# Graph network layers: rows shared by neighbouring rounds of scatters are given over from two chunks instead of one

## The chip, the cores and the metric

The kernel runs on one core of a Trainium2 chip. The metric is the time of one execution on the device in microseconds (us); lower is better. Engines are named as in the profile: PE (TensorE), DVE (VectorE), ACT (ScalarE), POOL (GpSimd), SP (SyncE). All but DVE and PE also issue transfers here.

## The reference, cut to what matters

There are 50000 nodes and 25000 edges, each with 128 features in fp32. Two graph layers run one after the other, each with a residual:

```python
edge_index = stack([src, dst])              # dst is sorted, src is random
h = relu(layernorm(x))
x = x + SAGE(h)                             # mean of h[src] over edges with the same dst, @ W_l.T, + h @ W_r.T
h = relu(layernorm(x))
agg = segment_sum(edge_attr_128, src, 50000)
h = concat([h, agg], axis=1)
h = bn(silu(h @ W1 + b1)); h = bn(silu(h @ W2 + b2))
x = x + (h @ W3 + b3)
```

`bn` takes its mean and variance over all nodes. Of this the change touches the segment sum of the second layer alone: rows of `edge_attr` are multiplied by the lower half of W1 and added at row `src[e]` of a table in DRAM, `acc2`.

## The kernel before, in words

**Tiling.** Nodes and edges go in 49 rounds, 0 to 48: 512 edges and 1024 nodes in each, the last with a shorter tail. A round is written (i, par) with r = 2i + par. Its 512 edges are four chunks, c0 to c3 here, of 128 rows. The phases are A (first layer), B (second layer's sums, and its first product), C (adds `acc2`, silu, statistics), F and G.

**Scatters of B.** `scatter_b(k)` (L837) issues four indirect DMAs on the POOL queue (L848). Each adds 128 rows of 128 floats to `acc2` at the rows in `target_b`. An add is a read and a write of DRAM, so two scatters that hold the same row must not be in flight together. Inside a round this can't be: equal rows are summed beforehand into one of them, and the others are sent to rows past the table (`count`, `mark`, `aim`: more than one match moves the target to a dump row). Between rounds it is kept in order by waits: c0 of a round waits until c0, c1 and c2 of the round before have landed (`s_sc2`, 48), and c1 waits until its c3 has landed (`s_end2`, 16). c0 needn't wait for that c3: a row that c3 shares with c0 of the next round is given over to it. `compare_carry` (L1170) finds such rows (`carried`, L1177) and moves their old target to the dump row; in `edge_product` (L1434) PE adds c3 of the round before, through `carried`, to c0 of the new round (L1440).

**One round of B on each engine.** POOL: the four scatters. DVE, `body_b` (L1279) for round r: eight adds x1 = acc1 times 1/degree + y (L1291), eight `bn_stats` (L1296), `bn_aggr` (L1302), then for round r + 2 `match` (four `scalar_tensor_tensor` of 128, 256, 384 and 512 columns, L1153) and the carry, then the targets of round r + 1 (`aim`, L1143), then the scales of round r (L1194, L1195). ACT, `body_b` (L999): normalise r (eight, L904), copy z of r - 1 (L992), copy the sums of r + 2 (L919), relu of r (L912), the root of r + 1 (L897), copy the product of r + 2 (`copy_v`, L925) into one of four buffers. PE, `round_b` (L1481): sums of r + 2 (L1430), transposes of r (L1422), `edge_product` of r + 2 (L1438, L1440), product of r (L1495).

**SP's queue of B**, `step_b` (L600) for round r, in this order: wait until c3 of r has landed (L603); load acc1 (L506) for round r + 2, and from round 32 on its y too (the stretch from there on is called spilled: y of the rounds before is still on the chip, and the results z of later rounds go out to DRAM from ACT's queue, L997); wait for DVE's adds of r; store x1 of r (L514); load the names and the edge rows for r + 4 (L585, L588).

Of the kernel before, what the change touches and what calls it, by code (L numbers as in the profile page):

```python
# [7 lines left out]
P = 128  # L8
ROWS = 4
# [5 lines left out]
def this(sem, par, i, inc=1):  # L15

    return sem[par], (i + 1) * inc


def two_ago(sem, par, i, inc=1):  # L20

    return sem[par], i * inc


def four_ago(sem, par, i, inc=1):

    return sem[par], (i - 1) * inc


def last(sem, par, i, inc=1):  # L30

    return sem[1 - par], (i + par) * inc


def gnn_layers(nc, x, src, dst, edge_attr, WlT, WrT, W1, b1, g1, be1, W2, b2, g2, be2, W3, b3, out):
# [90 lines left out]
    with ctx:  # L126
        def sb(name, shape, dt=fp32):
            return ctx.enter_context(nc.sbuf_tensor(name, shape, dt))
# [4 lines left out]
        def pair(name):  # L133
            return [sem(f"{name}_{k}") for k in range(2)]
# [27 lines left out]
        def part(shape, dt=fp32):  # L162
# [8 lines left out]
            if dt is not fp32:  # L171
# [29 lines left out]
        sumT = part([P, ROWS, P])  # L201
        irow = part([P, 2, ROWS, P])
        iota_c = part([P, COLS // 2]).bitcast(fp16)
        carried = [iota_c[:, :].bitcast(fp32)[:, 0:P], tabs[:, 2 * GROUP:2 * GROUP + P]]
        cols = part([P, 2, 4, ROWS])
        count = sb("count", [P, 2, ROWS])
        more = sb("more", [P, 2])
        alone = sb("alone", [P, 2])
        shift = sb("shift", [P, 2, ROWS])

        st6 = part([P, 2, 12, 6])
# [6 lines left out]
        hot_dve = [spare[:, 2 * ACT_H * P:(ROWS + ACT_H) * P].rearrange("p (j c) -> p j c", j=ROWS - ACT_H),  # L218
                   w2s[:, :].bitcast(fp16).rearrange("p (j c) -> p j c", j=ROWS - ACT_H)]
        bst = sb("bst", [P, 2 * (RF + 1), 6])  # L220
        zeros = bst[:, :, :].rearrange("p a s -> p (a s)")[:, 0:ZCOLS]
        row_stage = hT[:, 1, :, :].rearrange("p c d -> p (c d)")[:, 0:4 * P].rearrange("p (k c) -> p k c", k=4)
        bn = sb("bn", [P, 2, 8])
# [26 lines left out]
        def phase(tag, names):  # L250

            return {k: pair(f"{tag}_{k}") for k in names.split()}
# [5 lines left out]
        s_pre = pair("pre_rows_loaded")  # L258
        B = phase("b", common.replace(" stored", "") + " rows_loaded y_loaded a_loaded z_copied z_stored")
        x1_stored = [sem(f"b_x1_stored_{k}") for k in range(RING)]  # L260
        C = phase("c", "transposed added silu stats stored")
        F = phase("f", "product silu stats stored")
        G = phase("g", "scaled product done stored early_stored")

        acc2_loaded = [pair(f"acc2_loaded_{k}") for k in range(2)]
        x1_loaded = [pair(f"x1_loaded_{k}") for k in range(2)]
# [1 line left out]
        late_loaded = [sem(f"late_loaded_{r}") for r in range(2 * KEPT_LATER, RF + 1)]  # L268
        s_sc1 = pair("acc1_scattered")
        s_sc2 = pair("acc2_scattered")  # L270
        s_end2 = pair("acc2_last_chunk_scattered")
        s_set = sem("eps_then_zeros_then_names_set")
        s_fetched = sem("z_fetched")
# [149 lines left out]
        def x1_place(i, par):  # L423

            if type(i) is int and not 2 <= i < IT - 1:
                return (xin if i in (0, IT - 1) else res)[:, par, :, :]
            return kept(i - 2, par)
# [66 lines left out]
        def _(sp):  # L494
# [125 lines left out]
            sweep(sp, step_b, (KEPT,), wide=True, margin=2)  # L620


            sp.wait_ge(*this(s_sc2, 0, IT, 48))
            sp.wait_ge(*this(s_sc2, 1, IT - 1, 48))
            sp.wait_ge(*this(s_end2, 0, IT, 16))
            sp.wait_ge(*this(s_end2, 1, IT - 1, 16))
            for k in range(RING):
# [120 lines left out]

            def store_out(i, par, tail=False, early=False):
                sp.wait_ge(*this(G["done"], par, i))  # L750
                store_nodes(x1_place(i, par), out_v, 2 * i + par, tail, G["early_stored" if early else "stored"][par])

            def step_g(i, half, odd, par, early=False):

# [8 lines left out]
            doubled(sp, lambda *step: step_g(*step, early=True), 3, EARLY_G)  # L763
            doubled(sp, step_g, EARLY_G, EARLY_G + 4)
            for par in range(2):
                sp.wait_ge(G["early_stored"][par], 16 * EARLY_G)
            for i, par, tail in late_rounds():
                load_late(zy_dram, KEPT_LATER, i, par, tail, kept(i - KEPT_LATER, par))
            doubled(sp, step_g, EARLY_G + 4, KEPT_LATER)
# [13 lines left out]
        def _(pool):  # L783
# [53 lines left out]
            def scatter_b(k):  # L837

                i, par = k // 2, k % 2
                pool.wait_ge(*this(B["v_copied"], par, i))  # L840
                pool.wait_ge(*this(B["targets"], par, i))

                if k:
                    pool.wait_ge(*last(s_sc2, par, i, 48))
                for j in range(ROWS):
                    if k and j == 1:
                        pool.wait_ge(*last(s_end2, par, i, 16))
                    pool.indirect_dma_start(  # L848
                        acc2, bass.IndirectOffsetOnAxis(ap=target_b[:, k, j:j + 1], axis=0),
                        vrow_b[k % RING][:, j, :], None, compute_op=ALU.add)\  # L850
                        .then_inc((s_end2 if j == ROWS - 1 else s_sc2)[par], 16)

            def fetched_a(k):

# [25 lines left out]
        def _(act):  # L880
# [53 lines left out]
            def copy_v_b(i, par, tail, slot):  # L934
                if type(i) is int and i == 0:
                    act.wait_ge(*this(s_sc1, 1 - par, IT - 1 + par, 64))
                elif type(i) is int and i == 1:
                    act.wait_ge(*this(s_sc1, 0, IT, 64))
                else:
                    act.wait_ge(*four_ago(s_sc2, par, i, 48))  # L940
                    act.wait_ge(*four_ago(s_end2, par, i, 16))
                copy_v(B, vrow_b[slot], i, par, tail)

# [131 lines left out]
        def _(dve):  # L1075
# [59 lines left out]
            def link_(ins):  # L1135
                signal(ins)
                settle()
# [32 lines left out]
            def compare_carry(i, par, tail):  # L1170

                p = edge_parts(tail)
                before = 1 - par
                match(B, i, par, tail)
                if not (type(i) is int and i == 0):
                    dve.wait_ge(*two_ago(B["v_ready"], par, i))
                link_(nc.vector.scalar_tensor_tensor(  # L1177
                    carried[par][:, 0:p], irow[:, par, 0, 0:p], cols[:, before, 0, ROWS - 1:ROWS],
                    alone[:, before:before + 1].broadcast_to([P, p]), ALU.is_equal, ALU.mult,
                    accum_out=more[:, par:par + 1]))  # L1180
                nc.vector.tensor_scalar(alone[0:p, par:par + 1], count[0:p, par, ROWS - 1:ROWS], 1.5, None, ALU.is_lt)
                link_(nc.vector.scalar_tensor_tensor(
                    count[:, before, ROWS - 1:ROWS], more[:, par:par + 1], 2.0, count[:, before, ROWS - 1:ROWS],
                    ALU.mult, ALU.add))
                link_(mark(before, False))
                dve.sem_inc(B["compared"][par], 1)
# [79 lines left out]
            dve.wait_ge(*this(A["summed"], 1, IT - 1))  # L1266
            for par in range(2):
                link_(nc.vector.tensor_copy(cols[:, par, 0:2, :], src_tab[:, par, :, :]))
                if par:
                    compare_carry(0, par, False)  # L1270
                else:
                    link_(match(B, 0, par, False))
                    link_(nc.vector.tensor_scalar(alone[:, par:par + 1], count[:, par, ROWS - 1:ROWS], 1.5, None,
                                                  ALU.is_lt))
                    dve.sem_inc(B["compared"][par], 1)
            aim(B, 0, 0, False)
            done[0] += chain["n"]
            add_a(IT, 0, True, 2, 0)
            def body_b(before, now, after, ahead):  # L1279
                i, par, tail, spill, slot = now  # L1280
                r = 2 * i + par
# [117 lines left out]
        def _(pe):  # L1399
# [34 lines left out]
            def edge_product(w, par, tail, carry=None):  # L1434
                p = edge_parts(tail)
                for j in range(ROWS):
                    given = carry is not None and j == 0
                    ins = nc.tensor.matmul(psV[0:p, j, :], sumT[:, j, 0:p], w[:, :], start=True, stop=not given)  # L1438
                    if given:
                        ins = nc.tensor.matmul(psV[0:p, j, :], carried[par][:, 0:p], carry[:, ROWS - 1, :],  # L1440
                                               start=False, stop=True)
                return ins

            def round_a(i, par, tail):
# [30 lines left out]
            def multiply_edges_b(i, par, tail, _, slot):  # L1475
                pe.wait_ge(*this(B["sum_copied"], par, i))
                pe.wait_ge(*last(B["v_copied"], par, i))
                first = type(i) is int and i == 0 and par == 0
                edge_product(w1b, par, tail, None if first else vrow_b[(slot - 1) % RING]).then_inc(B["v_ready"][par], 1)

            def round_b(before, now, after, ahead):  # L1481
# [100 lines left out]
```

## Time and profile before

| | |
|---|---|
| median of 3 runs | 1505.77 us (1505.55 to 1508.4) |
| the profiled execution's own time | 1503.21 us |
| its span in the trace | 1501.3 us |
| mean granted TensorE clock | 0.918 |
| busy: PE, DVE, ACT, POOL | 68%, 73%, 57%, 55% of the span |

Busy shares are means over phases with different limits, so the phase that the change touches has to be read by itself. In the trace B's scatters run from 650.9 to 1132.2 us. The profiled execution is 2.56 us below the median. A landing time is counted from the start of the instruction that issues the transfer.

### The profile page before, as it was taken

The numbers are of one execution on the slowest core, as the hardware profiler recorded it, in microseconds if no ns is written. First come the engines' busy times: TensorE is split into PE (matmuls) and PEld (weight loads), VectorE is DVE, ScalarE is ACT, GpSimd is POOL, SyncE is SP. The second block draws the span as 40 slices with busy tenths as digits, with TensorE's granted clock in tenths as the row PEclk, the third lists the DMA queues.
The fourth block names the chain that finished last, engine by engine and source line by source line (L and its number), as shares of the span: only waits on it lengthen the run. The fifth ranks groups of instructions, "written<-read, shape, count | busy, mean of one in ns | idle before, by whom it ended". The sixth has DMA issues, their size and how long they took to land.

```text
span 1501.3 us, 22959 instructions
## 1 busy us (share of the span) xinstructions
PE 1021.5 (68%) x5247; PEld 726.3 (48%) x5247; DVE 1099.7 (73%) x4644; ACT 862.9 (57%) x1686; POOL 828.5 (55%) x601
## 2 busy tenths in 40 slices
PE   0237767677666667658777777776657877997866
PEld 0125555555544455435444444444435765446755
DVE  1438888888867766669788878776764877778978
ACT  0226777777755555537666666656564545665533
POOL 6778887888888888766666667655551000000000
PEclk9959999999999988969999999889997998999989
DMA  9988898877766666677777777899987996207999
GB/s 277 386 275 220 204 228 211 187 166 169 170 146 142 135 144 143 140 159 199 196 195 197 193 195 198 234 264 273 268 247 250 348 333 234 97 28 260 407 403 373
DMA packets 225365, 333.72 MB, mean 222 GB/s; under 512 B 35778, under 2 KB 87242, under 8 KB 225300
## 3 DMA queue, kind: packets, MB, share of 16 engines
q1 hardware_dynamic: 157516, 285.22, 56.1%
q0 software_dynamic: 62720, 38.57, 20.4%
q10 hardware_dynamic: 5064, 9.29, 1.7%
q14 instruction: 52, 0.43, 0.1%
q8 instruction: 13, 0.21, 0.1%
HBM read 179.20 MB, written 153.80 MB: 222 GB/s over the span
## 4 chain that ended last, share of the span: by engine, by line
POOL 41%; DMA 26%; issue 16%; PE 10%; DVE 5%; SPq 1%; ACT 1%; POOLq 0%; DVEq 0%; ACTq 0%
POOL acc L833 20%; POOL acc L848 11%; DMA acc<-zT,target_b 8%; DMA acc<-tabs,target_b 8%; POOL xin L811 7%; PE ps L1538 6%; POOL zT L819 4%; DMA zT<-x_dram 3%; DMA xin<-acc 2%; PE ps L1548 1%; DMA acc<-zT,tabs 1%; DVE zT L1383 1%; DVE zT L1387 1%; PE ps L1514 1%; PE ps L1517 1%
## 5 line engine op out<-in xcount | busy, mean ns | idle before, releaser
L1430 PE MATMUL ps<-zT 128*128 128x512 f32 (+5 forms) x784 | 278.0, 505 | 196.4 <-ACT zT L951 135.4
L833 POOL DMA_INDIRECT acc<-zT,tabs x196 | 314.8, 1606 | 71.5 <-issue 64.6
L1430 PEld LDWEIGHTS ps<-zT 128*128 128x128 f32 (+1 forms) x784 | 162.6, 217 | 338.8 <-issue 208.8
L848 POOL DMA_INDIRECT acc<-zT,target_b x100 | 161.0, 1610 | 87.1 <-DMA acc<-zT,target_b 32.5
L1153 DVE SCALAR_TENSOR_TENSOR zT<-zT 128x128 f32<-128x128 f32 (+3 forms) x392 | 192.9, 548 | 12.7 <-DMA zT<-row_dram 6.4
L1221 DVE BATCH_NORM_STATS2 zT<-zT 128x6 f32<-128x128 f32 (+1 forms) x384 | 78.9, 278 | 165.3 <-DMA zT<-in_x_dram 165.3
L848 POOL DMA_INDIRECT acc<-tabs,target_b x96 | 153.7, 1601 | 81.4 <-issue 32.0
L811 POOL DMA_INDIRECT xin<-in_x_dram,tabs x140 | 141.9, 1014 | 47.3 <-issue 42.4
L1422 PE MATMUL ps<-ident,zT 128*128 128x128 f32 (+1 forms) x784 | 111.5, 288 | 65.4 <-ACT zT L904 65.4
L1422 PEld LDWEIGHTS ps<-ident,zT 128*128 128x128 f32 (+1 forms) x784 | 92.2, 149 | 78.4 <-ACT zT L904 75.7
L1548 PE MATMUL ps<-w,hT 128*128 128x128 f32 (+1 forms) x784 | 101.5, 285 | 38.2 <-DVE zT L1387 28.7
L1328 DVE BATCH_NORM_STATS2 bst<-zT (+1 forms) x168 | 107.5, 682 | 23.7 <-ACT zT L1048 23.7
L1461 PE MATMUL ps<-wr,hT 128*128 128x128 f32 (+1 forms) x784 | 102.4, 287 | 32.3 <-DVE zT L1212 32.0
L1461 PEld LDWEIGHTS ps<-wr,hT 128*128 128x128 f32 (+1 forms) x784 | 98.6, 201 | 40.0 <-issue 37.4
L1548 PEld LDWEIGHTS ps<-w,hT 128*128 128x128 f32 (+1 forms) x784 | 94.0, 197 | 46.0 <-issue 46.0
L897 ACT ACTIVATE zT<-zT,eps 128x12 f32<-128x12 f32 x98 | 29.6, 302 | 150.0 <-DVE zT L1241 109.8
L904 ACT ACTIVATE zT<-zT 128x128 f32<-128x128 f32 (+1 forms) x288 | 115.3, 479 | 0.0
L904 ACT ACTIVATE zT<-xin,zT 128x128 f32<-128x128 f32 (+1 forms) x200 | 79.7, 480 | 59.1 <-DVE zT L1195 59.1
L912 ACT ACTIVATE hT<-ps 128x1024 f32<-128x1024 f32 (+1 forms) x100 | 99.6, 998 | 23.6 <-PE ps L1422 23.5
L904 ACT ACTIVATE zT<-res,zT 128x128 f32<-128x128 f32 (+1 forms) x198 | 78.8, 480 | 50.7 <-DVE zT L1195 50.7
L1495 PE MATMUL ps<-hT,w1a 128*128 128x512 f32 x196 | 101.4, 643 | 2.3 <-ACT hT L912 2.3
L1065 ACT ACTIVATE hT<-zT,bn 128x1024 f32 (+3 forms) x50 | 60.9, 1221 | 69.7 <-PE ps L1548 68.9
(159 smaller groups left out, 2017.0 us busy)
## 6 DMA issues: line engine op xcount, KB each, us to landing
acc<-bst SPq DMA_DIRECT2D x12, 2112.0 KB, 21.5
acc<-bst SPq DMA_DIRECT2D x48, 528.0 KB
zT<-row_dram SPq DMA_DIRECT2D x98, 256.0 KB, 5.7
zT<-in_x_dram SPq DMA_DIRECT2D x48, 512.0 KB, 6.7
zT<-acc SPq DMA_DIRECT2D x48, 512.0 KB, 4.3
zT<-x_dram SPq DMA_DIRECT2D x42, 512.0 KB, 8.5
out_dram<-zT SPq DMA_DIRECT2D x42, 512.0 KB, 7.7
zT<-in_edge_attr_dram SPq DMA_DIRECT2D x48, 256.0 KB, 6.4
```

Of the source, the lines that this page charges most:

```text
L811: pool.indirect_dma_start(row_ring[:, k % RING, j, :], None, x, bass.IndirectOffsetOnAxis(ap=icol[:, c:c + 1], axis=0)).then_inc(s_ring[k ...
L833: pool.indirect_dma_start(acc1, bass.IndirectOffsetOnAxis(ap=target_a[:, k, j:j + 1], axis=0), v[:, j, :], None, compute_op=ALU.add).then_ ...
L848: pool.indirect_dma_start(acc2, bass.IndirectOffsetOnAxis(ap=target_b[:, k, j:j + 1], axis=0), vrow_b[k % RING][:, j, :], None, compute_op ...
L904: ins = nc.scalar.activation(to[0:p, c, :], t[0:p, c, :], ACT.Identity, bias=nm[0:p, par, k:k + 1], scale=rs[0:p, par, k:k + 1])
L912: ins = nc.scalar.activation(hT[:, par, c, 0:p], psR[:, c, 0:p], ACT.Relu)
L1153: ins = nc.vector.scalar_tensor_tensor(same[0:p, par, at:at + j + 1, 0:p], irow[0:p, par, 0:j + 1, 0:p], cols[0:p, par, 0, j:j + 1], order ...
L1328: ins = nc.vector.bn_stats(bst[:, bass.ds((2 * i + par) * 2 + half, 1), :] .rearrange("p a s -> p (a s)"), place(i, par)[:, c, 0:p])
L1422: ins = nc.tensor.transpose(ps_t[:, c, 0:p], t[0:p, c, :], ident[0:p, 0:p])
L1430: ins = nc.tensor.matmul(psA[:, 0:j + 1, 0:p], t[0:p, j, :], same[0:p, par, at:at + j + 1, 0:p], start=(j == ROWS - 1), stop=(j == 0))
L1461: ins = nc.tensor.matmul(psQ[0:q, c, :], hT[:, par, c, 0:q], wr[:, :], start=True, stop=True)
L1495: ins = nc.tensor.matmul(psQ[:, c, 0:q], w1a[:, :], hT[:, par, c, 0:q], start=True, stop=True)
L1548: ins = nc.tensor.matmul(ps2[par][0:q, c, :], hT[:, par, c, 0:q], w3[:, :], start=True, stop=True)
```

## The change

It gives over the rows of two chunks. A row of c2 or c3 that is also in c0 of the next round, and a row of c3 that is also in c1, moves there. In turn c0 of a round waits for c0 and c1 of the one before (32), c1 waits for its c2 (a semaphore pair of its own, `s_mid2`), and c2 waits for its c3. `compare_carry` gets a second, 256 columns wide comparison; `edge_product` adds three given matmuls instead of one. The wide result lies in `bst`, whose first columns were the zeros that clear `acc2`, so DVE waits once for those copies (`s_zero2`). Rounds 0 and 1 hand nothing over, and round 1 waits for all of round 0. ACT and SP wait for `s_sc2` at 32 and `s_mid2` at 16 where they waited for `s_sc2` at 48. C's `stored` pair also counts the early stores of G.

```diff
-        carried = [iota_c[:, :].bitcast(fp32)[:, 0:P], tabs[:, 2 * GROUP:2 * GROUP + P]]
-        more = sb("more", [P, 2])
-        alone = sb("alone", [P, 2])
+        more = sb("more", [P, 2, 2])
+        alone = sb("alone", [P, 2, 2])
...
+        carried_2 = [iota_c[:, :].bitcast(fp32)[:, 0:P], tabs[:, 2 * GROUP:2 * GROUP + P]]
+        carried_3 = [bst[:, :, :].rearrange("p a s -> p (a s)")[:, k * 2 * P:(k + 1) * 2 * P]
+                     .rearrange("p (c q) -> p c q", q=P) for k in range(2)]
...
                 if k:
-                    pool.wait_ge(*last(s_sc2, par, i, 48))
+                    pool.wait_ge(*last(s_sc2, par, i, 32))
+                if k == 1:
+                    pool.wait_ge(*last(s_mid2, par, i, 16))
+                    pool.wait_ge(*last(s_end2, par, i, 16))
                 for j in range(ROWS):
-                    if k and j == 1:
+                    if k > 1 and j == 1:
+                        pool.wait_ge(*last(s_mid2, par, i, 16))
+                    if k > 1 and j == 2:
                         pool.wait_ge(*last(s_end2, par, i, 16))
                     pool.indirect_dma_start(
                         acc2, bass.IndirectOffsetOnAxis(ap=target_b[:, k, j:j + 1], axis=0),
                         vrow_b[k % RING][:, j, :], None, compute_op=ALU.add)\
-                        .then_inc((s_end2 if j == ROWS - 1 else s_sc2)[par], 16)
+                        .then_inc((s_sc2, s_sc2, s_mid2, s_end2)[j][par], 16)
...
 def compare_carry(i, par, tail):
...
                 match(B, i, par, tail)
-                if not (type(i) is int and i == 0):
-                    dve.wait_ge(*two_ago(B["v_ready"], par, i))
+                dve.wait_ge(*two_ago(B["v_ready"], par, i))
+                nc.vector.scalar_tensor_tensor(
+                    carried_3[par][:, :, 0:p], irow[:, par, 0:2, 0:p], cols[:, before, 0, ROWS - 1:ROWS],
+                    alone[:, before, 1:2].unsqueeze(2).broadcast_to([P, 2, p]), ALU.is_equal, ALU.mult,
+                    accum_out=more[:, par, 1:2])
                 link_(nc.vector.scalar_tensor_tensor(
-                    carried[par][:, 0:p], irow[:, par, 0, 0:p], cols[:, before, 0, ROWS - 1:ROWS],
-                    alone[:, before:before + 1].broadcast_to([P, p]), ALU.is_equal, ALU.mult,
-                    accum_out=more[:, par:par + 1]))
-                nc.vector.tensor_scalar(alone[0:p, par:par + 1], count[0:p, par, ROWS - 1:ROWS], 1.5, None, ALU.is_lt)
+                    carried_2[par][:, 0:p], irow[:, par, 0, 0:p], cols[:, before, 0, ROWS - 2:ROWS - 1],
+                    alone[:, before, 0:1].broadcast_to([P, p]), ALU.is_equal, ALU.mult,
+                    accum_out=more[:, par, 0:1]))
+                nc.vector.tensor_scalar(alone[0:p, par, :], count[0:p, par, ROWS - 2:ROWS], 1.5, None, ALU.is_lt)
                 link_(nc.vector.scalar_tensor_tensor(
-                    count[:, before, ROWS - 1:ROWS], more[:, par:par + 1], 2.0, count[:, before, ROWS - 1:ROWS],
+                    count[:, before, ROWS - 2:ROWS], more[:, par, :], 2.0, count[:, before, ROWS - 2:ROWS],
                     ALU.mult, ALU.add))
...
 def edge_product(w, par, tail, carry=None):
                 for j in range(ROWS):
-                    given = carry is not None and j == 0
-                    ins = nc.tensor.matmul(psV[0:p, j, :], sumT[:, j, 0:p], w[:, :], start=True, stop=not given)
-                    if given:
-                        ins = nc.tensor.matmul(psV[0:p, j, :], carried[par][:, 0:p], carry[:, ROWS - 1, :],
-                                               start=False, stop=True)
+                    taken_over = [] if carry is None or j > 1 else [(carried_3[par][:, j, :], ROWS - 1)]
+                    if taken_over and j == 0:
+                        taken_over.append((carried_2[par], ROWS - 2))
+                    ins = nc.tensor.matmul(psV[0:p, j, :], sumT[:, j, 0:p], w[:, :], start=True, stop=not taken_over)
+                    for same_row, chunk in taken_over:
+                        ins = nc.tensor.matmul(psV[0:p, j, :], same_row[:, 0:p], carry[:, chunk, :], start=False,
+                                               stop=(chunk == ROWS - 1 - len(taken_over) + 1))
...
+            link_(mark(0, False))
             aim(B, 0, 0, False)
...
+            dve.wait_ge(s_zero2, 16 * RF)
```

## Rows read from the trace of the kernel before

**Rows 1.** The chain of waits, in order of time: start, length, what.
```profile
847.09 4.39 DMA acc<-zT,target_b
...
852.28 1.54 POOL acc L848
```

**Rows 2.** Windows: length, busy of PE, PEld, DVE, ACT, POOL, clock, DMA share, GB/s.
```profile
682.86:955.69 272.83, 202.66 (x891) 127.98 (x892) 225.00 (x1205) 186.27 (x383) 186.88 (x116) 0.96 0.79 197
955.69:1126.66 170.97, 114.22 (x460) 72.44 (x458) 118.41 (x629) 102.22 (x207) 102.17 (x64) 0.89 0.89 259
25.00:100.00 75.00, 13.58 (x72) 9.81 (x72) 15.70 (x91) 14.30 (x33) 57.19 (x59) 0.88 1.04 386
```

**Rows 3.** Timeline of POOL: start, length, instruction, [idle before, what ended it].
```profile
842.90 1.54 POOL L848 DMA_INDIRECT acc<-zT,target_b  x1 [1.38 <-DMA acc<-tabs,target_b]
844.75 2.04 POOL L848 DMA_INDIRECT acc<-zT,target_b  x1 [0.30 <-issue]
847.09 1.54 POOL L848 DMA_INDIRECT acc<-zT,target_b  x1 [0.30 <-issue]
...
852.28 1.54 POOL L848 DMA_INDIRECT acc<-zT,target_b  x1 [1.79 <-DMA acc<-zT,target_b]
```

**Rows 4.** Timeline of POOL: c0 of rounds 1, 3, 32 and 48.
```profile
664.70 1.54 POOL L848 DMA_INDIRECT acc<-zT,target_b  x1 [6.64 <-DVE target_b L1143]
...
682.86 1.54 POOL L848 DMA_INDIRECT acc<-tabs,target_b  x1 [2.63 <-DMA acc<-tabs,target_b]
...
955.69 1.54 POOL L848 DMA_INDIRECT acc<-zT,target_b  x1 [3.24 <-DMA acc<-tabs,target_b]
...
1126.66 1.54 POOL L848 DMA_INDIRECT acc<-zT,target_b  x1 [1.69 <-DMA acc<-tabs,target_b]
```

**Rows 5.** L848, landing of the scatters, rounds 3 to 31, then 32 to 47.
```profile
DMA to landing us min/median/max: 3.3/5.3/7.8
...
DMA to landing us min/median/max: 3.8/6.1/8.2
```

**Rows 6.** Waits of DVE (us, times, longest), rounds 3 to 31, then 32 to 47.
```profile
DVE xin L1291 <- DMA zT<-acc: 16.2, 12, 2.8
DVE res L1291 <- DMA zT<-acc: 9.1, 9, 1.7
...
DVE xin L1291 <- DMA xin<-y_dram: 22.4, 8, 3.9
DVE res L1291 <- DMA res<-y_dram: 21.9, 8, 6.0
```

**Rows 7.** Timeline of DVE: match, 256 and 384 columns; adds; targets; next adds.
```profile
843.66 0.48 DVE L1153 SCALAR_TENSOR_TENSOR zT<-zT 128x256 f32<-128x256 f32 x1
...
844.07 0.61 DVE L1153 SCALAR_TENSOR_TENSOR zT<-zT 128x384 f32<-128x384 f32 x1
...
847.85 2.20 DVE L1291 SCALAR_TENSOR_TENSOR xin<-zT,rdeg 128x128 f32<-128x128 f32 x8 [0.96 <-DMA zT<-acc]
...
855.59 0.16 DVE L1143 TENSOR_TENSOR target_b<-shift,zT 128x4 f32 x1 [0.26 <-DVE shift L1162]
...
856.92 2.19 DVE L1291 SCALAR_TENSOR_TENSOR res<-zT,rdeg 128x128 f32<-128x128 f32 x8 [0.79 <-DMA zT<-acc]
```

**Rows 8.** Timeline, spilled stretch: a c3, the load behind it, the adds behind that.
```profile
1046.92 1.55 POOL L848 DMA_INDIRECT acc<-zT,target_b  x1 [0.30 <-issue]
...
1052.64 0.40 SPq L506 DMA_DIRECT2D zT<-acc  x1
...
1059.25 0.88 DVE L1291 SCALAR_TENSOR_TENSOR res<-zT,rdeg,res 128x128 f32<-128x128 f32 x3 [2.19 <-DMA res<-y_dram]
```

**Rows 9.** Timeline of PE and ACT around the given matmul of one round.
```profile
841.67 0.39 PE L1440 MATMUL ps<-zT,tabs 128*128 128x128 f32 x2
...
843.42 0.58 ACT L925 ACTIVATE zT<-ps 128x512 f32<-128x512 f32 x1
...
846.92 3.19 ACT L904 ACTIVATE zT<-xin,zT 128x128 f32<-128x128 f32 x8 [2.93 <-DVE zT L1195]
```

More of the change, by code:

```diff
@@ L260, in gnn_layers @@
         x1_stored = [sem(f"b_x1_stored_{k}") for k in range(RING)]
-        C = phase("c", "transposed added silu stats stored")
+        C = phase("c", "transposed added silu stats")
+        C["stored"] = pair("c_z_stored_then_g_early_out_stored")
         F = phase("f", "product silu stats stored")
-        G = phase("g", "scaled product done stored early_stored")
+        G = phase("g", "scaled product done stored")
         acc2_loaded = [pair(f"acc2_loaded_{k}") for k in range(2)]
@@ L270, in gnn_layers @@
         s_sc2 = pair("acc2_scattered")
+        s_mid2 = pair("acc2_third_chunk_scattered")
         s_end2 = pair("acc2_last_chunk_scattered")
@@ L620, in _ @@
             sweep(sp, step_b, (KEPT,), wide=True, margin=2)
-            sp.wait_ge(*this(s_sc2, 0, IT, 48))
-            sp.wait_ge(*this(s_sc2, 1, IT - 1, 48))
+            sp.wait_ge(*this(s_sc2, 0, IT, 32))
+            sp.wait_ge(*this(s_sc2, 1, IT - 1, 32))
+            sp.wait_ge(*this(s_mid2, 0, IT, 16))
+            sp.wait_ge(*this(s_mid2, 1, IT - 1, 16))
             sp.wait_ge(*this(s_end2, 0, IT, 16))
@@ L750, in store_out @@
                 sp.wait_ge(*this(G["done"], par, i))
-                store_nodes(x1_place(i, par), out_v, 2 * i + par, tail, G["early_stored" if early else "stored"][par])
+                store_nodes(x1_place(i, par), out_v, 2 * i + par, tail, (C if early else G)["stored"][par])
             def step_g(i, half, odd, par, early=False):
@@ L765, in _ @@
             for par in range(2):
-                sp.wait_ge(G["early_stored"][par], 16 * EARLY_G)
+                sp.wait_ge(C["stored"][par], 16 * (IT - KEPT_LATER + (0 if par else 2) + EARLY_G))
             for i, par, tail in late_rounds():
@@ L939, in copy_v_b @@
                 else:
-                    act.wait_ge(*four_ago(s_sc2, par, i, 48))
+                    act.wait_ge(*four_ago(s_sc2, par, i, 32))
+                    act.wait_ge(*four_ago(s_mid2, par, i, 16))
                     act.wait_ge(*four_ago(s_end2, par, i, 16))
@@ L1268, in _ @@
                 link_(nc.vector.tensor_copy(cols[:, par, 0:2, :], src_tab[:, par, :, :]))
[L1269 to L1275, printed above, removed]
+                link_(match(B, 0, par, False))
+                link_(nc.vector.tensor_scalar(alone[:, par, :], count[:, par, ROWS - 2:ROWS], 1.5, None, ALU.is_lt))
+                dve.sem_inc(B["compared"][par], 1)
+            link_(mark(0, False))
             aim(B, 0, 0, False)
@@ L1477, in multiply_edges_b @@
                 pe.wait_ge(*last(B["v_copied"], par, i))
-                first = type(i) is int and i == 0 and par == 0
+                first = type(i) is int and i == 0
                 edge_product(w1b, par, tail, None if first else vrow_b[(slot - 1) % RING]).then_inc(B["v_ready"][par], 1)
```

## The prediction

> **What bounds the kernel now.** I read the chain of waits first. In B it holds two things by turns, the instruction on POOL and the landing of its scatter, one such pair per round [rows 1]: a c2 starts at 847.09 and lands 4.39 us later, and the next scatter on the chain starts at 852.28, so 852.28 - 847.09 - 4.39 = 0.80 us lie between a landing and the scatter that waited. POOL's own timeline names the pieces [rows 3]: c0 at 842.90, c1 at 844.75, c2 at 847.09, and the next c0 at 852.28, after 1.79 us of idleness that a landing ended. The period is c0 to c2 (4.19), landing (4.39), restart (0.80): 9.38 us.
>
> How long B runs at that pace comes from the c0 of four rounds [rows 4]. Rounds 3 to 32 take 955.69 - 682.86 = 272.83 us, 9.41 a round over 29. Rounds 32 to 48, the spilled ones, take 170.97 us, 10.69 a round over 16. The median landing is 5.3 us in the first stretch and 6.1 in the second [rows 5], and that agrees with the longer period.
>
> Then the question is what stands right behind. POOL is busy 186.88 us for 116 scatters in the first stretch [rows 2], 1.61 each, so 6.44 a round; with three gaps of 0.30 [rows 3] and one of 0.80 it could go round in 8.1 us. DVE is nearer. Its waits for loads are 16.2 + 9.1 = 25.3 us over 29 rounds, 0.87 a round [rows 6], which leaves 9.41 - 0.87 = 8.54 of work and small links. Two neighbouring rounds give it directly [rows 7]: adds begin at 847.85, the next adds could have begun at 856.92 - 0.79 = 856.13, that is 8.28. I take 8.4. In the spilled stretch DVE waits 22.4 + 21.9 = 44.3 us, 2.8 a round, for y [rows 6]. The loads that it waits for are held on SP behind the landing of a c3 [rows 8], so this idleness too hangs on the scatters.
>
> **The change, part by part.**
>
> The waits of POOL. The two scatters between a c1 and the c0 that now waits for it are c2 and c3; before, one stood between. The chain of a round becomes c0 to c1 (1.85 [rows 3]), landing of c1, restart: 1.85 + 4.39 + 0.80 = 7.04 with this landing, 7.95 with the median of 5.3, 8.75 with the spilled median of 6.1. c1 behind c2 and c2 behind c3 have the same distance, so they are loops of the same length. A wait ahead of a scatter that is already met costs nothing that can be seen: c1 waits before the change, c2 doesn't, and both have a gap of 0.30 [rows 3]. Behind a late c1 on POOL's queue stand c2 and c3 of its round, and behind c3 SP's loads.
>
> DVE. A comparison of 256 columns is added. The 256 column match takes 0.48, and the next starts 0.41 after it [rows 7]; I charge 0.41, since they overlap. The small operations on two columns instead of one are charged nothing. DVE then needs 8.4 + 0.41 = 8.81 a round (8.69 to 8.95 by the two estimates). That is above POOL's 8.1 and above the scatter chain's 7.95: in the first stretch DVE becomes the bound. The load that DVE waits for now comes early, since the scatters pull ahead of it. The once-only wait for the zero copies is nothing: POOL passes the same wait ahead of its first scatter of B, and DVE first has to wait for acc1.
>
> PE. Two more matmuls per round. The given one of a round is two records that take 0.39 together at 841.67, so 0.8 more at most, between ACT's copy of the sums and `copy_v` at 843.42. ACT has 2.93 us of idleness before it may normalise at 846.92 [rows 9]; that covers it, and without that cover 0.8 would lengthen ACT's round.
>
> The start. c0 of round 1 waited 6.64 us for DVE's targets [rows 4], so the new comparison moves it by 0.41. Its waits for all of round 0 are covered by the same 6.64. From there to c0 of round 3 it was 18.16 us and is 2 x 8.81 + 0.41 = 18.03.
>
> The first stretch gives 29 x (9.41 - 8.81) = 17.4 us, with the start 17.5.
>
> The spilled stretch is where the size is open. Bound from below: the loop through SP. A c3 starts at 1046.92, the load behind it is issued at 1052.64 (5.72), the adds that need it start at 1059.25 (6.61) [rows 8]; adds to targets are 855.59 - 847.85 = 7.74 [rows 7] and now 8.15; restart 0.80; c0 to c3 three times 1.86. That is 26.86 us for three rounds, 8.95 each. Bound from above: no gain, 10.69, because the 16 DMA engines are the limit. Their share is 0.89 there [rows 2], 0.89 x 10.69 = 9.5 us of work a round. The highest share of a long stretch is 1.04 [rows 2], which would give 9.15; a full 1.0 gives 9.5. I take 9.4, near these: 16 x (10.69 - 9.4) = 20.6 us. In the first stretch the share is 0.79, 7.4 us a round, and doesn't bind.
>
> The Trainium skill (DMA: Bandwidth & Descriptors, Specifications) puts the limit of HBM at about 358 GB/s for a core. The rounds move 259 GB/s x 10.69 us = 2.77 MB [rows 2], so by that rule 7.7 us a round would do and the loop of 8.95 would bind, which makes the spilled gain 27.8. The row's share speaks for the dearer figure, and the sum keeps it.
>
> The same skill (SBUF — State Buffer, on the port pair that VectorE and GpSimd share) speaks against an added VectorE operation with two SBUF inputs: it can lock GpSimd out for its length. The longest scatter here is 2.04 against 1.54 [rows 3], so such a hit is some 0.5 us; 0.5 more on POOL's 8.1 stays below 8.81, and the sum doesn't change.
>
> Sum: 17.5 + 20.6 = 38.1 us off the profiled execution's 1503.21, 1465.1. The median of the runs is 2.56 higher, so 1467.7. C, F and G keep their work; the shared `stored` pair is only a count.
>
> **The rivals.** First, the loads eat the spilled gain: they are issued in one burst behind each c3, so landings grow as the period shrinks and 10.69 stays. For it: the share of 0.89, and landings up to 8.2 [rows 5]. Against: 1.04 was reached. Then only 17.5 remains: 1488.3.
>
> Second, it ends slower: three scatters in flight slow each other's read-and-add traffic. Place: landing of c1. Break-even is at a landing of 9.41 - 1.85 - 0.80 = 6.76 in the first stretch and 8.04 in the second, against 5.3 and 6.1 now. With landings a third longer, 7.07 and 8.13, periods are 9.72 and 10.78: 29 x 0.31 + 16 x 0.09 = 10.4 us slower, 1516. For it: the landing is already longer with more traffic. Against: spacing on POOL stays 1.85, so the rate of scatters rises by under a tenth.
>
> Third, nothing to measure: landings a quarter longer (6.63), or the wait doesn't bind as the chain says because SP's loads set the pace anyway and take the same time behind c3. The time stays within 0.2% (3 us, about what a measurement of this kernel can tell from no change), 1505.8. Against: in the first stretch DVE waits only 0.87 a round.
>
> **How the numbers follow.** Forecast 0.64, its own range 1456 to 1480; spilled stretch without gain 0.20; nothing 0.07; slower 0.09. The range for eight times in ten: low end with DVE at 8.69 (20.9 us) and the spilled loop at 8.95 (27.8), 1457, rounded out to 1455; high end with the spilled gain gone and DVE at 8.95 (13.4), 1492. Faster by over 0.2%: 0.84; within: 0.07; slower: 0.09.
>
> **What would show it.** Right: c0 of round 32 near 938, POOL's idleness before c0 ended by DVE's targets and not by a landing, DVE's waits for acc1 near zero in rounds 3 to 31, period 8.8. In the spilled stretch a period near 9.4, a DMA share near 1.0, and DVE still waiting some for y. Wrong: landings of 6.8 us or more in the first stretch, or POOL's idleness still ended by a landing (second rival); a spilled period of 10.5 or more with landings of 7 us (first); a DVE round of over 9.3 us of work, or PE's given matmuls late enough for `copy_v` to hold ACT, would break the step that made DVE's price 0.41.

## The result, and the profile after

The changed kernel takes 1501.48 us (15 runs) against 1505.55 for the kernel before in the same comparison: ratio 0.997, 95% interval 0.9956 to 0.9984. A second comparison gave 0.9961 (0.9938 to 0.9984). So it is faster, by 0.3 to 0.4%, 4 to 6 us. The forecast was a gain of 38 us, to 1468, with a range from 1455 to 1492. The profiled execution took 1498.6 us (span 1496.9), 3 below the median.

The windows of the two stretches of B, rounds 3 to 31 and 32 to 47, with the columns of [rows 2] (the first window opens 0.31 us ahead of the c0 of round 3):

```profile
681.88:953.04 271.16, 211.14 (x1010) 139.62 (x1009) 237.86 (x1258) 187.11 (x386) 185.86 (x117) 0.98 0.80 199
953.04:1118.68 165.64, 112.39 (x519) 72.77 (x518) 123.14 (x659) 97.61 (x198) 100.95 (x64) 0.96 0.96 264
```

POOL's timeline, the c0 of rounds 1, 3, 32 and 48, as in [rows 4]:

```profile
664.33 1.54 POOL L859 DMA_INDIRECT acc<-zT,target_b  x1 [7.07 <-DVE target_b L1155]
...
682.19 1.73 POOL L859 DMA_INDIRECT acc<-tabs,target_b  x1 [1.93 <-DMA acc<-tabs,target_b]
...
953.04 1.54 POOL L859 DMA_INDIRECT acc<-zT,target_b  x1 [3.34 <-DMA acc<-tabs,target_b]
...
1118.68 1.54 POOL L859 DMA_INDIRECT acc<-zT,target_b  x1 [0.96 <-ACT zT L936]
```

Rounds 3 to 32 take 953.04 - 682.19 = 270.85 us, 9.34 a round, where they took 9.41. Rounds 32 to 48 take 165.64, 10.35 a round, where they took 10.69. At the c0 of round 48 the gain is 1126.66 - 1118.68 = 8.0 us. The forecast had 8.81 and 9.4 for the two periods.

The landing of the scatters, first and second stretch, as in [rows 5]:

```profile
DMA to landing us min/median/max: 3.3/6.3/8.4
...
DMA to landing us min/median/max: 3.7/6.5/9.0
```

The medians went from 5.3 to 6.3 and from 6.1 to 6.5. They mix the four positions of a round, which are taken apart below. DVE's waits for the loads of acc1 in the first stretch, as in [rows 6]:

```profile
DVE res L1305 <- DMA zT<-acc: 6.0, 8, 1.6
...
DVE xin L1305 <- DMA zT<-acc: 3.2, 5, 0.9
```

They fell from 25.3 to 9.2 us, by 16.1; the 29 added comparisons at 0.41 take up 11.9 of that, and the stretch is 2.0 shorter. But DVE did not become the bound. What ended POOL's idleness ahead of the scatters of this stretch, beside the gaps of 0.30 (us, times), is a landing ahead of 29 of its 30 c0:

```profile
  DMA acc<-zT,target_b: 29.2, 14
  DMA acc<-tabs,target_b: 28.9, 15
```

What the chain now holds is the landing of c1 where it was c2's. From the chain of waits of the changed kernel, in order of time (start, length, what):

```profile
815.58 7.04 DMA acc<-zT,target_b
...
825.25 6.80 DMA acc<-tabs,target_b
...
834.68 6.97 DMA acc<-tabs,target_b
...
844.29 6.56 DMA acc<-zT,target_b
```

And the kernel before, at the same place; the fourth is in [rows 1], 4.39 us:

```profile
818.46 4.73 DMA acc<-zT,target_b
...
827.68 5.75 DMA acc<-tabs,target_b
...
838.07 4.03 DMA acc<-tabs,target_b
```

Over all of rounds 3 to 31 the landings on the chain are 4.74 us long before (mean of 28) and 6.65 after (mean of 29). **The wait moved back by one scatter, some 2.0 us, and the landing that it waits for got 1.9 us longer.**

Read one scatter at a time, the two traces tell the following landings (mean us from the start of the scatter; in brackets for how many scatters the trace tells it):

| | c0 | c1 | c2 | c3 |
|---|---|---|---|---|
| before, rounds 3 to 31 | 6.80 (15) | 5.64 (15) | 4.40 (15) | 3.66 (14) |
| changed, rounds 3 to 31 | 6.70 (29) | 6.66 (29) | 5.15 (15) | 3.79 (15) |
| before, rounds 32 to 47 | 7.16 (8) | 6.71 (8) | 5.79 (8) | 4.89 (8) |
| changed, rounds 32 to 47 | 5.47 (16) | 7.18 (16) | 7.64 (8) | 6.38 (8) |

So two things are in the 1.9 us. One is the position: a c1 is issued about 2 us ahead of its c2, but in the first stretch it landed only 0.77 us ahead of it before and 0.50 after (means of 15 rounds each). The other came with the change: c1's own landing went from 5.64 to 6.66 us. How much of that second part is real is open, since c0, c1 and c2 count on one semaphore in the kernel before, and its trace may tell c1's moment too early.

Why an awaited c1 lands so late is seen on SP and POOL together. SP's timeline (all five transfers are in B, the last is the next round's first):

```profile
813.85 0.40 SPq L510 DMA_DIRECT2D zT<-acc  x1
814.45 0.41 SPq L518 DMA_DIRECT2D x_dram<-xin  x1
815.13 0.36 SPq L589 DMA_DIRECT2D zT<-row_dram  x1
815.67 1.02 SPq L592 DMA_DIRECT2D zT<-in_edge_attr_dram  x1
824.05 0.40 SPq L510 DMA_DIRECT2D zT<-acc  x1
```

And POOL's, a c0 and the c3 of its round:

```profile
823.40 1.54 POOL L859 DMA_INDIRECT acc<-tabs,target_b  x1 [2.42 <-DMA acc<-zT,target_b]
...
829.45 1.55 POOL L859 DMA_INDIRECT acc<-tabs,target_b  x1 [0.30 <-issue]
```

SP sends its burst when a c3 lands, at 813.85: acc1, x1, names, edge rows, within 2.8 us. The c1 that was issued at 815.58 lands 7.04 later, at 822.62, 8.8 us behind the release of the burst. In the kernel before the burst of that round was released at 814.33, and the c2 issued at 818.46 landed at 823.19, 8.9 us behind it:

```profile
814.33 0.40 SPq L506 DMA_DIRECT2D zT<-acc  x1
```

Back in the changed kernel, the next c0 follows at 823.40, its c3 is issued at 829.45 and lands before 832.98, when SP sends again. So there is a loop: c3 lands, the burst goes out, the next scatters land only behind it, POOL restarts, and its c3 releases the next burst but one. The loop spans two rounds, and its parts can be added up from the means over rounds 3 to 31. Before: release to c2's landing 8.49, restart of POOL 0.82, c0 to c3 5.75, landing of c3 3.66, restart of SP 0.14; that is 18.86, or 9.43 a round. After: release to c1's landing 8.21, then 0.82, 5.73, 3.79 and 0.13; that is 18.68, or 9.34 a round. The awaited landing comes only 0.28 us earlier behind the release, although it is c1's now and was c2's. So which of the two POOL waits for hardly matters in this loop. The experiments test it.

### The profile page after: what moved, and what is told of

Same layout as the page of the kernel before. It is cut to its first block, busy times and chain, and to the rows that moved or that the text cites. A ratio compares the mean times of both kernels' runs of the same rounds, so it can differ in the third digit from the quotient of the medians.

```text
span 1496.9 us, 23454 instructions
## 1 busy us (share of the span) xinstructions
PE 1033.5 (69%) x5433; PEld 745.5 (50%) x5433; DVE 1118.7 (75%) x4735; ACT 862.2 (58%) x1686; POOL 826.7 (55%) x601
## 4 chain that ended last, share of the span: by engine, by line
DMA 33%; POOL 31%; issue 13%; PE 11%; DVE 6%; SPq 5%; ACT 1%; DVEq 0%; POOLq 0%; ACTq 0%
POOL acc L839 20%; DMA acc<-zT,target_b 10%; DMA acc<-tabs,target_b 10%; POOL xin L817 6%; PE ps L1554 6%; POOL acc L859 5%; SPq L560 3%; DMA zT<-x_dram 3%; DMA xin<-acc 2%; DMA acc<-bst 2%; PE ps L1564 1%; DMA acc<-zT,tabs 1%; PE ps L1530 1%; DVE zT L1397 1%; DVE zT L1401 1%
## 5 line engine op out<-in xcount | busy, mean ns | idle before, releaser
L1444 PE MATMUL ps<-zT 128*128 128x512 f32 (+5 forms) x784 | 272.1, 497 | 179.5 <-ACT zT L963 129.6
L1511 PE MATMUL ps<-hT,w1a 128*128 128x512 f32 x196 | 96.4, 615 | 2.5 <-ACT hT L923 2.5
```

Of the source, the lines that this page charges most:

```text
L1444: ins = nc.tensor.matmul(psA[:, 0:j + 1, 0:p], t[0:p, j, :], same[0:p, par, at:at + j + 1, 0:p], start=(j == ROWS - 1), stop=(j == 0))
L1511: ins = nc.tensor.matmul(psQ[:, c, 0:q], w1a[:, :], hT[:, par, c, 0:q], start=True, stop=True)
```

## The experiments

Theory 1 is that loop. Theory 2 was the second rival: scatters in flight slow each other. Theory 3: the added work on DVE and PE gives the gain back.

The two traces already speak on theory 2. In the changed kernel's first stretch the next c0 starts 0.30 us after c2 has landed and 0.21 us before c3 has (means of 15 rounds); in the kernel before, it starts 0.32 us after c3 has landed (14 rounds). So the scatters of two rounds are in flight together for a fifth of a us, and of the two behind the awaited c1 only c3 still is when the next c0 starts. In the spilled stretch it is otherwise: there the next c0 starts 1.4 us ahead of c2's landing and 2.1 us ahead of c3's (7 rounds), and theory 2 stays open.

Each comparison is with the kernel before on the same chip and in the same session. It took 1520.6 us beside the versions with the old waits, with no wait of SP (both) and the changed kernel's light burst; 1518.7 beside the changed kernel again, its wait behind the load, its heavy burst and the light burst of before; and 1507.0 beside the wait for c2 and the heavy burst of before. The periods are read as above, from POOL's c0 of rounds 3, 32 and 48; those of the kernel before are from the trace ahead of the prediction, those of the changed kernel from its second trace.

| version | us (runs) | ratio to before | 3 to 31 | 32 to 47 |
|---|---|---|---|---|
| before | | 1 | 9.41 | 10.69 |
| changed | 1514.12 (12) | 0.9961 | 9.37 | 10.32 |
| changed, old waits | 1521.23 (12) | 1.0001 (0.9982 to 1.0019) | 9.49 | 10.63 |
| before, SP doesn't wait | 1554.77 (4) | 1.0212 (1.0183 to 1.0242) | 10.71 | 11.01 |
| changed, SP doesn't wait | 1489.45 (4) | 0.9788 (0.9764 to 0.9812) | 9.01 | 9.76 |
| changed, SP waits for c2 | 1490.82 (4) | 0.9884 (0.9835 to 0.9933) | 9.00 | 10.55 |
| changed, wait behind the load | 1531.37 (4) | 1.0083 (1.006 to 1.0107) | 9.63 | 11.12 |
| before, light burst | 1475.98 (1) | one run, 42.7 us below | 8.58 | 9.63 |
| changed, light burst | 1488.58 (1) | one run, 32.0 us below | 9.01 | 9.62 |
| before, heavy burst | 1592.55 (1) | one run, 85.5 us above | 11.22 | 13.17 |
| changed, heavy burst | 1566.57 (1) | one run, 47.9 us above | 10.96 | 10.58 |

**The changed kernel again.**

> The changed kernel once more, beside the others of this call. All theories: 2 to 6 us below the kernel before, as in the first result. It serves to set what SP's wait is worth against the changed kernel itself on one chip.

As expected: 4.6 us below the kernel before, and the same periods as in the first trace within 0.03.

**The added work with the old waits.**

```diff
                 if k:
                     pool.wait_ge(*last(s_sc2, par, i, 32))
-                if k == 1:
                     pool.wait_ge(*last(s_mid2, par, i, 16))
+                if k == 1:
                     pool.wait_ge(*last(s_end2, par, i, 16))
                 for j in range(ROWS):
                     if k > 1 and j == 1:
-                        pool.wait_ge(*last(s_mid2, par, i, 16))
-                    if k > 1 and j == 2:
                         pool.wait_ge(*last(s_end2, par, i, 16))
```

> The changed kernel with its added comparison and matmuls, but with the waits of before (c0 waits for c0, c1 and c2 of the round before, c1 for its c3). This prices the added work alone. Theory 1: DVE's 0.87 us of idleness per round covers 0.41, so 0 to 3 us above the kernel before, 1505 to 1509. Theory 3: the work isn't covered, 0.41 us x 48 rounds or more, 1520 and above, and the new waits would be worth 20 us.

The ratio is 1.0001. The comparison and the two matmuls are covered, and theory 3 falls. The landings on the chain of rounds 3 to 31 are 4.79 us there (mean of 29), as in the kernel before, so it is the new waits that bring the longer ones.

**A lighter burst**, in both kernels. It leaves out three quarters of the acc1 rows and of the edge rows; the names are loaded in full, so the scatters go to the same rows.

```diff
-                load_nodes(aux[:, par, :, :], acc1_v, r, tail, B["a_loaded"][par])
+                if tail:
+                    load_nodes(aux[:, par, :, :], acc1_v, r, tail, B["a_loaded"][par])
+                else:
+                    sp.dma_start(aux[0:32, par, :, :].rearrange("p (n j) d -> p n (j d)", n=2), acc1_v[0][r][0:32])\
+                        .then_inc(B["a_loaded"][par], 16)
...
-                sp.dma_start(rows[0:p, par, :, :].rearrange("p j d -> p (j d)"), ea_v[1] if tail else ea_v[0][r])\
+                q = p if tail else 32
+                sp.dma_start(rows[0:q, par, :, :].rearrange("p j d -> p (j d)"), ea_v[1] if tail else ea_v[0][r][0:q])\
```

> The changed kernel with a lighter burst in B: of the acc1 rows and the edge rows of a round only the first 32 partitions are loaded (the rest of the tiles keeps old values, and the output with it), 576 KB of some 1536 less. SP's order and waits stay. Theory 1: the burst is some 2 us shorter, landings of c1 fall by 1 to 2 us (to about 5), and the period to DVE's 8.8 or 8.9; time near 1480. Theory 2: landings of c1 stay above 6.3 us. Theory 3: landings fall but the period stays at 9.3.

> The kernel before with the lighter burst (acc1 rows and edge rows of a round loaded into the first 32 partitions only, so the output keeps old values there). Theory 1: its c2 lands behind the burst too, so landings of c2 fall by 1 us or more and rounds 3 to 31 go from 9.41 to 8.5 to 8.8 us without any of the change; time some 25 to 40 us below the kernel before. Theory 2: the landings don't hang on the loads, the period stays above 9.2.

In the kernel before, the landings on the chain of rounds 3 to 31 fell from 4.74 to 4.10 us (mean of 24), by 0.64 where 1 or more was expected:

```profile
781.35 3.85 DMA acc<-zT,target_b
...
789.81 4.05 DMA acc<-tabs,target_b
...
807.15 4.83 DMA acc<-zT,target_b
```

Its first stretch runs at 8.58 without any of the change, 0.83 below 9.41. The changed kernel comes to 9.01, and there, from 697.1 to 954 us, POOL's idleness before the scatters is ended by DVE's targets 22 times and by a landing 4 times (us, times):

```profile
  DVE target_b L1160: 37.6, 22
...
  DMA acc<-zT,target_b: 2.7, 2
  DMA acc<-tabs,target_b: 2.6, 2
```

So with the burst out of the way DVE is the bound, as forecast, and the change then makes the round longer: 9.01 against 8.58, 0.43 more. Theory 2 had the landings of c1 stay above 6.3 us and bound the round; with POOL waiting for targets, they don't bound it.

**A heavier burst**, in both kernels.

```diff
+    idle_dram = nc.dram_tensor("idle_dram", (RF, P, ROUND), fp32).ap()
...
                     load_b_nodes(*ahead)
+                if not tail:
+                    sp.dma_start(idle_dram[2 * i + par].rearrange("p (n c) -> p n c", n=2), x_v[0][2 * i + par])\
+                        .then_inc(s_w, 16)
...
+            sp.wait_ge(s_w, 16 * (13 + RF))
```

> The changed kernel with a heavier burst: beside the load of acc1, SP copies 512 KB of x to an unused table in DRAM in each round of B; nothing computes with it. Theory 1 (the round is a loop: c3 lands, the burst goes out, the scatters land behind it): the 256 packets more, at 0.08 us each over 16 engines, are 1.3 us more per round, and period and landing of c1 rise by as much: rounds 3 to 31 from 9.3 to 10.6 us, the time by 50 to 70 us. Theory 2 (scatters slow each other): the DMA engines are idle a fifth of the round, so the landings of c1 stay below 7.2 and the time rises by less than 20 us.

> The kernel before with the heavier burst (512 KB more per round, to an unused table). Theory 1: the loop through SP was there before the change too, so the same 1.3 to 1.6 us come on top of 9.41: rounds 3 to 31 at 10.7 to 11.1 us, as in the changed kernel with that burst (10.96), and the change is worth nothing there. Theory 2: only landings of c0 matter here, the period stays below 10.

The chain of the changed kernel with it:

```profile
789.52 8.89 DMA acc<-tabs,target_b
...
812.27 8.59 DMA acc<-zT,target_b
```

The first stretch goes from 9.37 to 10.96 (+1.6) with the change and from 9.41 to 11.22 (+1.8) without. The loop was expected to add 1.3, and 1.3 to 1.6 in the kernel before, and the change to be worth nothing; it is worth 0.26. The landings on the chain of the changed kernel went from 6.65 to 8.30 us (means of 29), as much as its period. The expectation missed the second stretch: before 10.69 to 13.17, changed 10.32 to only 10.58. DVE's waits for y, in the kernel before with the heavy burst from 1020 to 1200 us, and in the changed one from 1020 to 1180:

```profile
DVE res L1296 <- DMA res<-y_dram: 33.0, 8, 5.6
DVE xin L1296 <- DMA xin<-y_dram: 22.4, 6, 4.5
```

```profile
DVE res L1310 <- DMA res<-y_dram: 20.4, 8, 5.6
DVE xin L1310 <- DMA xin<-y_dram: 13.1, 7, 2.2
```

Here the change is worth 2.6 us a round, and why so much more than without the heavy burst (0.34) was not settled. In the kernel before with the heavy burst c2 lands 2.4 us behind c1 in this stretch (8 rounds), but 1.5 us in the first (14 rounds), where the change is worth 0.26; so that gap alone doesn't set it. The granted clock also differs, 0.81 before and 0.95 changed, but the chain of the kernel before holds only scatters and landings there, no matmul.

**SP doesn't wait for c3**, in both kernels.

```diff
-                sp.wait_ge(*this(s_end2, par, i, 16))
                 if ahead:
                     load_b_nodes(*ahead)
```

> The changed kernel; SP no longer waits for c3 of round r before it loads acc1 (and y) for r + 2, so these loads go out when DVE's adds of r free the buffer. Theory 1 (a loop through SP: the landing of c3 releases a burst of loads and stores, and the next round's scatters land only behind that burst): landings of c1 fall from 6.75 us towards 5.5, rounds 3 to 31 go from 9.34 to about 8.9 us, where DVE bounds, and the time is 1480 to 1492. Theory 2 (three scatters in flight slow each other, whatever else moves): landings of c1 stay at 6.3 to 7 and the time within 3 us of 1501. Theory 3 (the added work on DVE and PE gives the gain back): no change either.

> The same edit on the kernel before. Theory 1: its c2 also lands behind the burst, so the period of rounds 3 to 31 falls below 9.41, to 9.0 or 9.2, and the time to 1490 to 1500. Theories 2 and 3: no change, 1502 to 1508.

The changed kernel gains more than expected: 0.9788, 31.2 us below the kernel before, where 1480 to 1492 beside 1505.6 was 14 to 26 below. The first stretch is at 9.01, where 8.9 was expected. DVE doesn't wait for loads there any more (in the whole first stretch its largest wait ahead of the adds is 4.1 us of mere issue), and in the spilled stretch the DMA share is 1.02 over 100 us, with 9.76 a round:

```profile
DVE res L1304 <- issue: 4.1, 7, 0.7
...
1000.00:1100.00 100.00, 77.26 (x359) 53.62 (x358) 85.93 (x460) 68.48 (x141) 64.59 (x41) 0.93 1.02 297
```

It beats both kernels, the one before by 2.1%. But the landings on its chain stayed long, 6.54 us in the first stretch (mean of 25), where 5.5 was expected, and POOL's idleness there is still ended by a landing 26 times. They no longer release the loads, so they cost less. Two things changed at once here: the release, and the shape of the burst. SP now stands 24 times for DVE ahead of the names and 23 times for PE ahead of the edge rows, so its transfers leave one by one. Which of the two counts for more this run doesn't tell.

The kernel before goes the other way, 1.0212, and here the expectation was wrong in sign: theory 1, as it was written down, did not foresee it. The waits of ACT and DVE, 700 to 950 and 697 to 1000 us (us, times, longest):

```profile
ACT zT L924 <- DMA acc<-zT,target_b: 28.7, 8, 4.9
ACT tabs L924 <- DMA acc<-tabs,target_b: 26.2, 7, 4.9
...
DVE zT L1193 <- ACT zT L896: 32.6, 15, 5.3
```

L924 is `copy_v`: it waits until the scatters of four rounds ago have left its buffer. Without SP's wait DVE and the loads run ahead of the scatters (DVE does 1322 instructions from the c0 of round 3 to that of round 32, against 1205), the scatters fall behind, and ACT stands 54.9 us for a buffer; DVE then waits for ACT's root. The granted clock falls too, from 1.00 in 700 to 800 us to 0.83 in 800 to 1000, but the chain of that stretch holds scatters and landings and no matmul. So, as these waits read, SP's wait is a useful brake in the kernel before; no run tests that by itself, for instance with more buffers. In the changed kernel the same wait is a loss. The change alone moves the time by -0.4%, SP's edit alone by +2.1%, both together by -2.1%.

**SP's wait one transfer later.**

```diff
-                sp.wait_ge(*this(s_end2, par, i, 16))
                 if ahead:
                     load_b_nodes(*ahead)
+                sp.wait_ge(*this(s_end2, par, i, 16))
```

> The changed kernel; SP's wait for c3 stands behind the loads of acc1 (and y) and ahead of the store of x1 and the loads of names and edge rows, so that the burst is cut in two, and only the second part is released by c3. Theory 1: the first part leaves ahead of c3's landing, the second is half as long, so landings of c1 fall below 6.2 and the period to 9.0; time as without the wait, 25 to 35 us below the kernel before. Theory 2: no change against the changed kernel.

A miss: 1.0083. SP's timeline shows that the burst wasn't cut:

```profile
810.43 0.41 SPq L518 DMA_DIRECT2D x_dram<-res  x1
811.12 0.36 SPq L589 DMA_DIRECT2D zT<-row_dram  x1
811.66 0.56 SPq L592 DMA_DIRECT2D zT<-in_edge_attr_dram  x1
812.40 0.40 SPq L510 DMA_DIRECT2D zT<-acc  x1
```

All else being ready, SP goes straight from the edge rows to the next acc1. The four leave together behind c3 as before, with acc1 now last. The idea of half a burst was not tested by this run; it only shows that the same burst in another order is worse.

**SP waits for c2.**

```diff
-                sp.wait_ge(*this(s_end2, par, i, 16))
+                sp.wait_ge(*this(s_mid2, par, i, 16))
```

> The changed kernel; SP waits for the landing of c2 of the round instead of its c3 before it sends the burst. Theory 1: c2 and c3 both land at the end of the burst of the round before, c2 only 0.3 to 0.9 us earlier (5.3 + 846.15 = 851.5 against 851.8 in the first trace), so the loop gets shorter by that much at most: rounds 3 to 31 at 9.1 to 9.3 us, the time 0 to 10 us below the changed kernel (1514 beside a before of 1519), not near the version without the wait. If the place of the wait on POOL's chain alone counted, the time would not move at all.

Better than expected: 9.00 in the first stretch, and 16 us below the kernel before. The sizes in the expectation took c2 and c3 to land together whatever happened. But c2 is issued a scatter earlier than c3, and here it lands 1.9 us ahead of it (15 rounds). Estimated from this trace's means, the loop is 8.38 (release to c1's landing) + 0.82 + 3.73 (c0 to c2) + 3.89 (landing of c2) + 0.14, half of which is 8.5, below DVE's round of 9.0. So DVE is the bound: in rounds 3 to 31 POOL's idleness is ended by targets 19 times and by a landing 9 times. From its timeline:

```profile
808.41 1.54 POOL L859 DMA_INDIRECT acc<-zT,target_b  x1 [1.59 <-DVE target_b L1155]
...
817.20 1.54 POOL L859 DMA_INDIRECT acc<-tabs,target_b  x1 [1.57 <-DVE target_b L1155]
```

and SP's release comes at 806.75 and 815.61, 1.6 us ahead of the c0 instead of beside it:

```profile
806.75 0.40 SPq L510 DMA_DIRECT2D zT<-acc  x1
...
815.61 0.40 SPq L510 DMA_DIRECT2D zT<-acc  x1
```

The spilled stretch didn't gain (10.55 against 10.32). That the first stretch's loop closes through SP's wait is thereby shown a third way, with traffic, work and the scatters' own waits unchanged.

## Why the prediction was wrong, point by point

- *What bounds B now:* right as far as it went. Landings of scatters end POOL's idleness, DVE is next. What the prediction knew of SP, that its loads are held behind c3, it used for the loads alone. It did not see that the awaited scatters in turn land behind these loads.
- *"The chain of a round becomes c0 to c1 (1.85), landing of c1, restart: 1.85 + 4.39 + 0.80 = 7.04 with this landing, 7.95 with the median of 5.3":* this is the step that failed. The landing of the newly awaited scatter was taken from a c2, or from a median over all four positions, and held fixed under the change. Measured, a c1 of the changed kernel lands in 6.66 us, so the chain is 1.85 + 6.66 + 0.80 = 9.31, and that is the period of 9.34. Reading c1 by its position would not have been enough: with the 5.64 that the trace of before tells for it the chain is 8.29, still below DVE's 8.81, and the forecast would have stood. What the sum had no term for is that an awaited scatter lands behind the burst, 8.2 to 8.5 us after its release, and that the burst is released by the scatters' own c3. The second rival named the break-even, a landing of 6.76. Its place was right, and its mechanism is not what the first stretch shows.
- *DVE at 8.81 becomes the bound:* not reached in the changed kernel. Where DVE waits for no load (light burst, no wait of SP, wait for c2) the period is 9.00 or 9.01. The added 0.41 was right (9.01 - 8.58 = 0.43); the round of before was 8.58, so of the two estimates 8.54 was close, and 8.28, read from a single pair of rounds, too low.
- *PE's 0.8 is covered, the start costs 0.41:* the old-waits version at 1.0001 says that all added work is covered. The start came out a little earlier, not later (c0 of round 1 at 664.33, before at 664.70).
- *The port pair:* nothing of it is seen. The rule of the Trainium skill (SBUF — State Buffer, Who interferes with whom) is for a VectorE operation with two SBUF inputs beside a GpSimd instruction that reads SBUF. No run here shows whether the scatters' instructions do. The 116 scatters of rounds 3 to 31 kept POOL busy for 185.86 us, 1.60 each (the 117th in the row above only begins at the window's end), against 1.61 before.
- *The first stretch, 17.4 us:* it gave 272.83 - 270.85 = 2.0.
- *The spilled stretch, 9.4 a round, 20.6 us:* it gave 5.3, with 10.35. The loop through SP was computed at 8.95 with the landing of a c3 and a load of before, the same mistake: the landing of c3 went from 4.89 to 6.38 us in this stretch (8 scatters each), and c1 too waited for a landing, its c2's, in 5 of the 16 rounds. As a limit of the DMA engines 9.4 was not far off: 9.76 at a share of 1.02 without SP's wait. The limit of HBM that the Trainium skill gives (DMA: Bandwidth & Descriptors, Specifications, about 358 GB/s for a core) was not reached: that trace moved 297 GB/s at a full share, so the share was the better guide, as the sum had it. Nor is the figure a ceiling in this kernel: the third window of [rows 2] moved 386 GB/s, and there the measurement decides.
- *C, F and G keep their work:* yes, but 3.6 us of B's 8.0 were lost by the end. SP's timeline has C's first load at 1139.45 before and 1130.86 after, the chain has the first fold of the statistics at 1263.12 and 1258.34:

```profile
1139.45 0.93 SPq L506 DMA_DIRECT2D res<-acc  x2
```

```profile
1263.12 2.82 DVE bn L1355
```

```profile
1130.86 0.94 SPq L510 DMA_DIRECT2D res<-acc  x2
```

```profile
1258.34 2.82 DVE bn L1369
```

  That is 123.7 us and 127.5. The chain of the kernel before goes through the last scatters and C's first load. That of the changed kernel leaves the scatters at 1102.64 and goes by a load of y (9.94 us from 1103.07), the last rounds on DVE, ACT and PE, and a store of z (7.37 us from 1134.19) to a load of C at 1142.44. So the scatters no longer end B. What would give the 3.6 us back was not tried.
- *The rivals:* the first (no gain in the spilled stretch) and the third (nothing to measure) each hold a part. The third's reason, "SP's loads set the pace anyway", comes nearest to the truth and got 0.07. Its landing, 6.63 us, is also what was measured (6.66). The time moved a little more than its 0.2%, since the spilled stretch gained 5.3 us.
- *The signs of being wrong:* one of the two of the second rival was seen, POOL's idleness still ended by a landing, ahead of 29 of 30 c0. The landings of c1 stayed just short of the other, 6.8 us.

## What to carry to other kernels

When a wait is moved to an older transfer, read landings by position, not as a median: here scatters issued 2 us apart beside one burst landed 0.5 to 0.8 us apart, so the older one had mostly waited longer. That alone does not save the forecast. Look for what the landings themselves release. If they release traffic that the next transfers land behind, the loop goes through that release; measure from the release to the awaited landing and add up the whole loop. It is at the release that an edit paid here: the slack gained on the scatters was worth 0.4% alone and 2.1% once the release was taken off it. Try such an edit in the kernel at hand, since on the kernel before the same edit cost 2.1%.

## What was not expected of the hardware

- Landing by position in a round is far from even. In the changed kernel's first stretch the shortest landing is 3.3 us and the longest 8.4, for four equal scatters of 128 rows issued some 1.9 us apart; by position the means run from 6.70 (c0) to 3.79 (c3).
- Removing a wait made the kernel before 2.1% slower with the same work and traffic.
- The same kernel before took 1505.6, 1520.6, 1518.7 and 1507.0 us in four comparisons, so only ratios within one can be read. In the group with 1520.6 round 1 of B already began 15 us later (680.0 against 664.7, in the version with the old waits).
